# An expert's weights in one transfer instead of three, and one expert's load moved ahead of a store

## What is computed

```python
h = tokens(x)                                   # patches, layer norms, a 1024 -> 512 product
h = h + bitlinear_mlp(layernorm(h))             # 512 -> 2 x 1408 -> 512, weights of -1, 0, 1
x = layernorm(h)                                # 448 x 512, the input of the experts
probs = softmax(x @ router_w.T)                 # 32 experts
rw, sel = top_k(probs, 8);  rw = rw / sum(rw)   # 8 experts per token
for e in range(32):
    w_e = sum(where(sel == e, rw, 0), axis=-1)  # zero for tokens that did not pick e
    hid = silu(x @ w_gate[e]) * (x @ w_up[e])   # 512 -> 192, twice
    acc += hid @ w_down[e] * w_e[:, None]       # 192 -> 512
return h + acc
```

## Time and profile before

| what | us |
|---|---|
| median of 3 runs | 308.67 |
| lowest and highest of them | 306.58, 308.88 |
| the profiled execution | 307.58 |
| its span, first to last instruction | 305.8 |
| TensorE busy in the span | 279.5 |
| VectorE (DVE) busy | 151.0 |
| GpSimd (POOL) busy | 126.4 |
| ScalarE (ACT) busy | 125.1 |

### The profile page before, as it was taken

One profiled execution on the slowest core, in us unless ns is written; L12 is line 12 of the kernel. 1 busy time (PEld: TensorE's weight loads), 2 busy tenths in 40 slices (PEclk: granted clock), 3 DMA queues, 4 the chain that ended last, 5 costly groups with the idle time before them and its releaser, 6 DMA issues.

```text
span 305.8 us, 3907 instructions
## 1 busy us (share of the span) xinstructions
PE 279.5 (91%) x1159; PEld 147.4 (48%) x1159; DVE 151.0 (49%) x446; ACT 125.1 (41%) x213; POOL 126.4 (41%) x130
## 2 busy tenths in 40 slices
PE   4899999779999889999999999999989999949991
PEld 1435444455557355655465556555645554533231
DVE  2648999995988523343523333323323322303364
ACT  2347998999974221332133213321322232211101
POOL 4062211976521422246435643464355446443310
PEclk9999999999998699999999999999999999997997
DMA  7999999503998298799999999999999999974883
GB/s 251 332 424 417 381 405 309 189 0 120 336 316 281 52 294 292 259 269 331 341 316 313 352 327 313 323 327 312 310 342 335 301 316 337 324 171 65 162 217 124
DMA packets 27798, 85.51 MB, mean 280 GB/s; under 512 B 4209, under 2 KB 4337, under 8 KB 26785
## 3 DMA queue, kind: packets, MB, share of 16 engines
q1 hardware_dynamic: 19760, 64.78, 61.0%
q0 software_dynamic: 7488, 18.42, 25.2%
q10 hardware_dynamic: 530, 2.08, 2.6%
HBM read 72.34 MB, written 12.92 MB: 279 GB/s over the span
## 4 chain that ended last, share of the span: by engine, by line
PE 39%; DVE 18%; DMA 17%; issue 8%; POOL 4%; ACT 3%; POOLq 0%; DVEq 0%; ACTq 0%
PE ps L1163 17%; DMA scrap<-token_rows,idx 9%; PE ps L1192 7%; DMA sum<-w_t,add_idx 5%; PE ps L1184 4%; PE ps L1195 4%; DMA ring<-sum 3%; DVE big L1443 2%; POOL sum L647 2%; DVE stats L1327 2%; PE ps L1050 2%; DVE raw L1449 2%; PE ps L1217 1%; PE ps L1147 1%; DVE hit L1625 1%
## 5 line engine op out<-in xcount | busy, mean ns | idle before, releaser
L633 POOL DMA_INDIRECT scrap<-token_rows,idx x36 | 35.9, 996 | 83.2 <-DVE idx L1628 46.8
L647 POOL DMA_INDIRECT sum<-w_t,add_idx x32 | 51.3, 1604 | 28.1 <-issue 11.5
L866 ACT ACTIVATE w_t<-ps 128x512 f32<-128x512 f32 x36 | 21.4, 597 | 85.0 <-PE ps L1184 84.8
L1644 DVE COPY w_t<-ps 128x256 f32<-128x256 f32 x34 | 14.4, 425 | 58.8 <-PE ps L1220 45.5
L1639 DVE SCALAR_TENSOR_TENSOR w_t<-ps,scrap,w_t 128x192 f32<-128x192 f32 x32 | 13.2, 413 | 57.1 <-issue 47.3
L871 ACT ACTIVATE w_t<-ps 128x192 f32<-128x192 f32 x34 | 11.2, 330 | 55.9 <-PE ps L1163 50.7
L1163 PE MATMUL ps<-ring,w_t 128*128 128x384 f32 x96 | 33.1, 487 | 0.7 <-ACT w_t L866 0.7
L1184 PE MATMUL ps<-ident,scrap 128*128 128x128 f32 x144 | 24.2, 292 | 10.1 <-DMA scrap<-token_rows,idx 6.6
L555 POOL TENSOR_TENSOR root_out<-root_in,minus_half 112x1 f32<-112x1 f32 x20 | 13.1, 654 | 46.3 <-DVE root_in L1344 46.2
L954 PE MATMUL ps<-raw,last 128*112 128x512 f32 x64 | 31.1, 639 | 0.0
L1163 PE MATMUL ps<-big,w_t 128*128 128x384 f32 x88 | 30.2, 486 | 0.0
(11 more groups left out here) (214 smaller groups left out, 470.6 us busy)
## 6 DMA issues: line engine op xcount, KB each, us to landing
big<-in_ffn_gate_up SPq DMA_DIRECT2D x15, 768.0 KB
ring<-in_ffn_gate_up SPq DMA_DIRECT2D x13, 768.0 KB
raw<-in_ffn_gate_up SPq DMA_DIRECT2D x6, 768.0 KB
last<-in_ffn_gate_up SPq DMA_DIRECT2D x6, 768.0 KB
big<-in_ffn_w_down SPq DMA_DIRECT2D x15, 256.0 KB
ring<-in_ffn_w_down SPq DMA_DIRECT2D x13, 256.0 KB
big<-in_mlp_w_in SPq DMA_DIRECT2D x2, 1536.0 KB, 17.7
big<-in_mlp_w_in SPq DMA_DIRECT2D x2, 1280.0 KB, 20.2
```

The lines of the kernel that those rows point to most:

```text
L633: nc.gpsimd.indirect_dma_start(got[:, got_at(s), :], None, rows_dram[:, :], bass.IndirectOffsetOnAxis(ap=idx[:, s:s + 1], axis=0)).then_in ...
L647: nc.gpsimd.indirect_dma_start(acc_dram[m.two][:, :], bass.IndirectOffsetOnAxis(ap=add_idx[:, m.eight:m.eight + 1], axis=0), y[:, m.four, ...
L866: nc.scalar.activation(x_t[:, m.two, :, :], bank(2 + m.two).rearrange("p (c t) -> p c t", c=4), ACT.Copy).then_inc(xt_ready, 1)
L1644: nc.vector.tensor_copy(h_t[:, m.two, :, :], bank(6)[:, 0:2 * P].rearrange("p (c t) -> p c t", c=2)).then_inc(ht_ready, 1)
```

## The change

The host lays out the weights in one array `in_ffn` with a row of 2560 fp32 for each expert and partition: gate, up, the upper down rows, and a last part of 512 columns. For an even expert this last part holds its own 64 lower down rows in rows 0 to 63, and those of the next, odd expert in rows 64 to 127. So:

- In the main loop an even expert is one transfer of 128 rows of 10240 B, which brings the odd neighbour's lower rows too, and an odd expert is one of 128 rows of 8192 B. `down_two` reads the odd tile's lower rows from the even slot (`pair_rest_of`). All of it counts on `ld_gu`; `ld_dn` and TensorE's wait for it in `down_two` are gone.
- A load now waits for `y_done` alone: the even expert's for both experts of the pair that used the slots before, the odd one's for the same pair. The earlier start of the gate and up load on `gu_done` is gone.
- A picked expert is two transfers instead of three: 128 rows of 8192 B, and 64 rows of 2048 B (semaphore `ld_rest`). Its wait for `gu_done` is gone too.
- Expert 10 is issued right after the four row stores, once `z_done` is full, and no longer behind the store of shares and `xt_done`. Expert 11 stays where it was.

```diff
@@ tile and list counts
-    def down_loaded(self, u):
-        return 32 * self.k + 32 * ((NE + 4 * self.i + u) // R + 1)
+    def rest_loaded(self):
+        return 16 * self.k + 16
...
+        def pair_rest_of(n):
+
+            return slots[n - n % 2][rest_rows(n), WG + D:WCOLS]
...
@@ SP
-            def load_gate_up(e, n):
-                sp.dma_start(slots[n][:, 0:WG], we_gate_up[e, :, :]).then_inc(ld_gu[n], 16)
-
-            def load_down(e, n):
-                sp.dma_start(down_of(n), we_down[e, 0:P, :]).then_inc(ld_dn[n], 16)
-                sp.dma_start(down_rest_of(n), we_down[e, P:IE, :]).then_inc(ld_dn[n], 16)
-
             def load_expert(t):
-                load_gate_up(t, t)
-                load_down(t, t)
+
+                n, cols = t % R, WCOLS if t % 2 == 0 else WG + D
+                sp.dma_start(slots[n][:, 0:cols], ffn[t, :, 0:cols]).then_inc(ld_gu[n], 16)
+
+            def load_picked(e, n):
+
+                sp.dma_start(slots[n][:, 0:WG + D], ffn[e, :, 0:WG + D]).then_inc(ld_gu[n], 16)
+                sp.dma_start(down_rest_of(n), ffn[e, 0:IB, WG + D:WCOLS]).then_inc(ld_rest[n], 16)
...
+            sp.wait_ge(z_done, NG)
+            load_expert(10)
             sp.wait_ge(gate_ready, NG)
             sp.dma_start(rows_v[:, :, D:ROW], rows[:, :, D:ROW]).then_inc(rows_out, 16)
-            sp.wait_ge(z_done, NG)
             sp.wait_ge(xt_done, 1)
-            load_expert(10)
             load_expert(11)
             for t in range(R, NE):
-                sp.wait_ge(gu_done, t - R + 1)
-                load_gate_up(t, t % R)
-                sp.wait_ge(y_done, t - R + 1)
-                load_down(t, t % R)
+                sp.wait_ge(y_done, t - R + (1 if t % 2 else 2))
+                load_expert(t)
...
-                    sp.wait_ge(gu_done, R * k + (NE - R + n + 1))
-                    load_gate_up(bass.ds(e, 1), s)
                     sp.wait_ge(y_done, R * k + (NE - R + n + 1))
-                    load_down(bass.ds(e, 1), s)
+                    load_picked(bass.ds(e, 1), s)
...
@@ TensorE, down_two and down_lists
-                    pe.wait_ge(ld_dn[m.slot], 2 * m.loaded())
...
-                    nc.tensor.matmul(bank(4 + m.two), h_t[rows_, m.two, 1, :], down_rest_of(m.slot), start=False, stop=True
+                    nc.tensor.matmul(bank(4 + m.two), h_t[rows_, m.two, 1, :], pair_rest_of(m.slot), start=False, stop=True
...
-                            pe.wait_ge(ld_dn[n], m.down_loaded(u))
+                            pe.wait_ge(ld_rest[n], m.rest_loaded())
```

More of the change, by code:

```diff
@@ L104, in pairs_of, with program @@
         yield k, n_pairs
-def program(nc, x, w_tok, vecs, gb1, w_in, w_down, g_down, w_router, we_gate_up, we_down, out):
+def program(nc, x, w_tok, vecs, gb1, w_in, w_down, g_down, w_router, ffn, out):
     rows_dram = nc.dram_tensor("token_rows", (ROWS, ROW), F32).ap()
@@ L315, in program @@
         ld_gu = [sem(f"ld_gu{n}") for n in range(R)]
-        ld_dn = [sem(f"ld_dn{n}") for n in range(R)]
+        ld_rest = [sem(f"ld_rest{n}") for n in range(R)]
         ld_got = [sem(f"ld_got{n}") for n in range(8)]
@@ L1765, in laid_out @@
     import numpy as np
+    rest = np.zeros((NE, P, D), we_down.dtype)
+    rest[:, 0:IB] = we_down[:, P:IE]
+    rest[0::2, IB:P] = we_down[1::2, P:IE]
     return {
@@ L1775, in laid_out @@
         "in_router_w": w_router.T.reshape(DC, 128, NE).transpose(1, 0, 2).reshape(128, DC * NE),
-        "in_ffn_gate_up": np.concatenate([w.reshape(NE, P, 4 * IE) for w in (we_gate, we_up)], axis=2),
-        "in_ffn_w_down": we_down,
+        "in_ffn": np.concatenate([w.reshape(NE, P, 4 * IE) for w in (we_gate, we_up)] + [we_down[:, 0:P], rest], axis=2),
     }
```

## The result

| | before | after |
|---|---|---|
| median | 307.62 us (306.16 to 308.88, 4 runs) | 318.86 us (317.76 to 322.86, 4 runs) |
| profiled execution | 307.58 | 317.76 |
| its span | 305.8 | 316.0 |

The ratio is 1.036, interval 1.028 to 1.043: slower by 3.6%. I had forecast 303.0 us, range 298.5 to 309.5, and given "slower" 0.12. Single executions that ran more than 1.5% above the fastest of their kernel count in the medians of this document, and are left out of its ratios and intervals.

The account below looks back on a forecast made before the run. DMA was taken as the slower of two full resources, 10.6 us a pair against TensorE's 9.9, its backlog growing. 307.58 - 2.8 - 2.5 + 0.3 = 302.6 us, median put at 303.0, range 298.5 to 309.5.

Parts of the forecast that it names:

- Step (1): Main loop: one transfer for three, without the 64-row piece, brings pairs to 9.9 us; -2.8 us (bounds 0 and -3.8).
- the rival of the long packets: Main loop: longer rows in SP's queue hold up the indirect queue, scatters land later; 307 to 316 us, chance 0.07.
- Step (3): SP's loads: gate-up now waits for the down product, adding contention but no late tile; counted 0 (bounds 0 and +2.4).
- Step (4): Before the loop: expert 10 issued ahead of the gate store, which loses little; +0.3 us (bounds 0 and +1.0).
- Step (2): TensorE's last wait for a gather, ended at 274.25: scatter and gather land sooner; -2.5 us (bounds 0 and -4.5).
- POOL's own order places that gather: Sign at the last gather: pairs at 9.9 and last wait still 4 us mean POOL's order, not the landing, places it.

Follow-up runs that it names:

- x_rows3: x_rows2 with rows of 3 KB for gate and up and of 4 KB for an even expert's down part; 301.93 us, ratio 0.987 to the kernel before.
- a_rows2_64: a_rows2 with the 64-row piece back in the main loop; 310.40 us, ratio 1.011 to the kernel before.
- a_rows2: The changed kernel with weights laid out in HBM as rows of 2 KB, same transfers, order and waits; 306.56 us, ratio 1.002 to the kernel before.
- b_rows2: The kernel before with gate and up weights in rows of 2 KB instead of 6 KB; 304.94 us, ratio 0.9945.
- x_rows2: a_rows2 with the gate and up load on gu_done again as its own transfer, and expert 10 late; 302.38 us, ratio 0.986 to the kernel before.
- b_late: The kernel before with gate and up loads waiting for y_done, three transfers and rows of 6 and 2 KB kept; 308.57 us, ratio 1.007.
- a_rows2_no10: a_rows2 with expert 10 loaded late again; 304.46 us, ratio 0.9945 to the kernel before.
- a_no10: The changed kernel with expert 10 loaded late again, where it was before; 317.60 us, ratio 1.036 to the kernel before.
- a_spread: The changed kernel with a pair's two transfers started about 5 us apart, main loop only; 314.27 us, ratio 1.023 to the kernel before.

## Why the prediction was wrong

**The reading of the kernel before held.** Two resources at the limit, the gather as the thing late, 3.8 us of the loop and 4.46 at its end to be had. x_rows3 took back the first in full and a third of the second.

**Step (1), relief for the engines, was right as a mechanism.** It shows for the 64-row piece. I had put the full-row rate as one end and 9.9 us a pair as the likely value. With and without that piece the full windows show 310 against 350 GB/s (a_rows2_64, a_rows2) and 314 against 352 (b_rows2, x_rows2), and a_rows2 runs at 9.86 us a pair, x_rows3 at 9.94. The page that I cited (the Trainium skill, SBUF — State Buffer, Door 1: The DMA port swizzle) is borne out by these windows in direction. The size is larger than my estimate from it: a pair's 3.44 MB take 11.0 us at 314 GB/s and 9.8 at 352, 1.2 us less where the estimate was 0.6. (352 is no upper end: a pair each 9.86 us, TensorE's pace, asks for only 349 GB/s.) In after itself the relief never showed in the pairs.

**The step that failed is the rival of the long packets,** to which I gave 0.07 and of which I said that rows speak against it. In one microsecond the indirect queue had moved 76 packets against 26. That stretch, 186 to 187 us, lay 2.6 us behind the handover of 183.36 in the kernel before, so it was the moment that decides; but it held rows of 6 and 2 KB, and I carried it to rows of 8 and 10 KB, which no stretch of the trace shows beside a scatter. So the sum took 5.3 us off for (1) and (2) and had nothing for scatters and gathers that land later. Instead nine pairs took 101.7 us where they had taken 93.1. In after the queues go nearly one for one from 148 to 151 us, 91 packets to 97, as the cited rule of the Trainium skill (DMA: Bandwidth & Descriptors, Queues, rings and completion order) would have it with one row a packet. For 3 us before that it is far worse, 14 to 81. And one for one isn't what rows of every length give: a_rows2 has 159 to 297 from 148 to 151 us. The prediction priced a scatter's eight rows at 1.2 us more and the scatter cycle at 11.3; the chain after has cycles of 12.2, 11.7 and 10.7 us, and the pairs take 11.3. So even the price was in the rival: "the scatter cycle goes from 10.1 to 11.3 us over eight pairs, +8". That the two figures agree is partly luck, because the rival had the rows take turns throughout and knew nothing of the 3 us in which the indirect queue nearly stood. The loss also began with the fourth pair of the loop and not in its last eight, and the measured 318.86 us lies above the rival's 307 to 316.

**The sum also let a term of relief stand for a term of latency.** I reasoned that if the engines need less time for the weights, the gathers land sooner. In after SP's queue took 55.7% of the engines' time instead of 61.0%, and the scatters beside a burst landed later. For the small transfers that others wait for here, how busy the engines were on the whole said nothing; what SP's queue had just been handed did.

**Step (3), the gate and up load,** counted at 0 with a bound of +2.4, costs about 2 us with rows of 6 KB (b_late, 1.007). With short rows a_rows2_no10 at 0.9945 and x_rows2 at 0.986 point to as much, across two calls. The mechanism was the named one: queue at the end of the loop, no late weights. I should have booked it, because at the last gather nothing swallows it.

**Step (4), expert 10,** counted at +0.3 with a bound of +1.0, costs 1.0: the store took 3.16 us instead of 2.2. After's first part ran 0.7 us ahead at that point (store issued at 99.47, has 100.18), so the first gather was only 0.24 late. In a_no10 it started at 103.55 us, in after at 103.57, and both ratios are 1.036. The reading that this store is what POOL waits for last was right. With short rows it shows in the time, 1.002 against 0.9945.

**Step (2), the last wait,** I put at 2 us; it was 3.17 in after and 3.0 to 4.1 with short rows. Pairs at 9.86 us with a last wait of 4.1, as in a_rows2, are what I had listed as a sign that POOL's own order places that gather; no run changed that order.

**What stays open.** Why SP's rows pass a waiting scatter for 3 us after a handover is not shown. From 145 to 148 us some 80 long rows went ahead, 5 for each engine, about 2.5 us of its time (82.6% of the 3 us). A fixed number of rows in line in front of each engine would explain a shorter stop with shorter rows, but a_rows2 doesn't give the same number: in its thinnest microsecond, 147 to 148 us, it has 19 packets to 148, nine rows for each engine. The traces show only starts of packets, not the lines in front of the engines. Row length and layout in HBM changed together in a_rows2, so an effect of the layout isn't excluded by that run alone; the steps from 2 to 10 KB, with layouts of several kinds, speak for the length. Nor is it settled how much of the loss is the burst: a_spread says a third, with overlapping intervals. And why 4 KB came out a little better than 2 KB was not looked into.

## What to carry to other kernels

Where a bulk load shares the DMA engines with small transfers that others wait for, try rows of 2 to 4 KB for the bulk, by the layout in HBM. That can keep the number of transfers and cost no time here, while rows of 8 and 10 KB cost 3.6%. Spread a load over all 128 partitions, as with the lower rows of two experts side by side (352 against 314 GB/s). And don't carry a queue's share that was read beside rows of one length over to longer ones: look for a stretch that has them, right after a handover, or count the step as open in the sum.

## What the runs showed that I had not expected

- The indirect queue nearly stopped: 14 packets from 2 to 5 us after a handover beside rows of 10 KB, against 121 beside rows of 2 KB with the same bytes handed over in the same burst.
- Length has a bend. Longest rows of 2 and 4 KB gave ratios 1.002 and 0.995, 6 KB 1.001, 8 KB 1.026, 8 and 10 KB 1.036.
- A wait of 2.52 us cost TensorE another 1.5 us, because its granted clock fell to 0.50 behind it.
- A store of 56 KB behind a load of 1.3 MB took 3.16 us with rows of 10 KB and 3.42 with rows of 2 KB to land, against 2.2, though the load had been issued 4.4 us before it (95.03 and 99.47 us in after). A second transfer before it moved the first gather to 106.30 us, and the idle TensorE then ran its first eight gate and up products in 4.55 us instead of 2.86.
